# A state-space layer and feed-forward layer on one core: the round loop written out, and GpSimd's normalisation by two whole-tile operations

## The chip, the cores and the metric

One core of a Trainium2 chip runs the whole program. The metric is the device time of one execution in microseconds (us), the median over repeated runs. An execution is also profiled once; its span runs from the first to the last instruction.

## What is computed

The input has 32 sequences of 256 tokens with 128 features, all in 32-bit floats. Cut to what matters, the reference is:

```python
def _layernorm(x, axis=-1, eps=1e-05):
    m = jnp.mean(x, axis=axis, keepdims=True)
    v = jnp.var(x, axis=axis, keepdims=True)
    return (x - m) / jnp.sqrt(v + eps)
...
            def step(h, inp):
                dt_t, Bt, Ct, xt = inp
                dA = jnp.exp(dt_t[..., None] * A)
                h = dA * h + (xt * dt_t)[..., None] * Bt[:, None, :]
                y = jnp.einsum('bdn,bn->bd', h, Ct)
                return (h, y)
...
        h = jax.nn.silu(_tlin(x, w1_w, w1_s)) * _tlin(x, w2_w, w2_s)
        h = jax.nn.gelu(_tlin(h, h1_w, h1_s), approximate=False)
        h = jax.nn.gelu(_tlin(h, h2_w, h2_s), approximate=False)
        return _tlin(h, w3_w, w3_s)
    x = L0_attn_x
    x = _layernorm(x + _L0_attn_ref(x, ...), axis=-1)
    x = _layernorm(x + _L0_ffn_ref(x, ...), axis=-1)
```

The first half (`_L0_attn_ref`) projects each token to 256 channels and a gate z, runs a causal convolution of four taps and a silu, derives B, C and a step size dt per token, runs the scan `step` over time with 16 states for each of 256 channels, gates the sum with silu(z) and projects back to 128. The second half is a gated layer of width 512, two hidden layers of 512 and a last projection. A layer norm follows each half. The two layer norms are what the second part of the change touches.

## The kernel before, in words

The 8192 tokens are cut into 16 blocks of 512 (`NB` = 16, two sequences each). A block passes through a software pipeline of rounds; `run(j, par, scan, intake, front, back, tail)` is written once for each engine and issues that engine's part of round j. Round j does five things side by side, each switched by a flag:

- scan of block j: 32 tiles of channel and state in 16 steps v of two. ScalarE makes dA by an exponential (L337), VectorE multiplies (L593, U) and scans (L600, hb), GpSimd multiplies by C (L322, pb), TensorE adds the products up in PSUM by transposes (L692, Y).
- intake of block j+2: projection (L655), the convolution's first tap (ScalarE, L347) and the others (VectorE, L542).
- front of block A = j+1: silu, rows of B and C to DRAM and their broadcast back by DMAs on SyncE's queue, and dt: ScalarE (L380, L386, L388), then GpSimd's addition `add_dt` (L260) at step 11, then GpSimd's product xd (L266) and ScalarE's copy of it into the bank X (L343).
- back of block F = j-1: gate, output projection, residual r1 (VectorE, L616), the first layer norm, the transpose of its result x1 (TensorE, L744), the copy x1T (ScalarE, L488), the gated layer and the first hidden layer (TensorE L711, L714, L707).
- tail of block T = j-2: second hidden layer, last projection (L729), residual r2 (VectorE, L641), the second layer norm, the store of yo by SyncE (L238).

Every engine runs its own instructions in order, and the order around the change is written by hand: each `if v == ...` says at which step of the scan a piece stands. All dependencies are semaphores. A `wait_ge` stands ahead of the instruction that needs it and holds all that follows on that engine.

**The loop.** `rounds(eng, run)` (L164) calls `run` for rounds 0 and 1 with Python numbers, then opens a hardware loop `eng.Fori` of (16 - 4) / 2 = 6 turns with two rounds each (rounds 2 to 13), then rounds 14 to 17 written out. In the loop j is a register, so the numbers that are waited for are computed from it. There are five jumps from a turn's end back to its beginning, after rounds 3, 5, 7, 9 and 11, and each engine makes its own.

**The normalisation.** A block's layer norm works on a tile of 128 partitions x 4 rows (`NT` = 4, for a partition's four tokens) x 128 features. VectorE makes mean and variance (`stats`, L557 and L562, into mv). GpSimd's `normalise` (L283) then calls `rsqrt` (add eps, L279; power -0.5, L281), waits for its result, and works through the four rows one by one: each is one `tensor_scalar` (L288) that subtracts the mean and multiplies by the scale, both of them one number for each partition. It is called at step 4 of a round for block F (result x1, wanted by TensorE's `turn_x1` at step 5), and at step 10 for block T (result yo, wanted by the store). In round 17 VectorE normalises the last block itself (L634), so GpSimd does 31 normalisations.

What stands behind the step-10 call on GpSimd: the product of step 10, `add_dt` at step 11, the product of step 11. ScalarE waits for `add_dt` ahead of the first gelu (L399) of step 12.

Of the kernel before, what the change touches and what calls it, by code (L numbers as in the profile page):

```python
# [10 lines left out]
P = 128  # L11
# [25 lines left out]
def build(nc, xT, xtok, win, wx, chp, wout, w1, w2, h1, h2, w3, scales, w3s, ident_in, out):  # L37
    with ExitStack() as ctx:
# [6 lines left out]
        def sem(name):  # L45
            return ctx.enter_context(nc.semaphore(name))
# [58 lines left out]
        s_win, s_chp, s_ident, s_wx, s_weights = (sem("s_win"), sem("s_chp"), sem("s_ident"), sem("s_wx"),  # L105
                                                  sem("s_weights"))
        s_b0, s_pre0, s_soft0, s_dt0 = sem("s_b0"), sem("s_pre0"), sem("s_soft0"), sem("s_dt0")
        s_ready = sem("s_ready")
        s_zero, s_aexp, s_aneg, s_w3s = (sem("s_zero"), sem("s_aexp"),
                                                        sem("s_aneg"), sem("s_w3s"))  # L110
        s_xT, s_xtok = sem("s_xT"), sem("s_xtok")
# [12 lines left out]
        s_ga, s_sg, s_up, s_upc, s_hid = sem("s_ga"), sem("s_sg"), sem("s_up"), sem("s_upc"), sem("s_hid")  # L124
        s_h1, s_g1, s_h2, s_g2, s_w3 = sem("s_h1"), sem("s_g1"), sem("s_h2"), sem("s_g2"), sem("s_w3")
        s_w3t, s_r2t = sem("s_w3t"), sem("s_r2t")
        s_r2, s_l2, s_rs2, s_yo, s_out = sem("s_r2"), sem("s_l2"), sem("s_rs2"), sem("s_yo"), sem("s_out")

        def halves(x):
# [31 lines left out]
        def bank_in(b, c):  # L161
            return BIN_EARLY[c] if isinstance(b, int) and b < 2 else BIN[c]

        def rounds(eng, run):  # L164

            run(0, 0, True, True, True, False, False)
            run(1, 1, True, True, True, True, False)
            with eng.Fori(0, (NB - 4) // 2) as i:  # L170
                run(i * 2 + 2, 0, True, True, True, True, True)
                run(i * 2 + 3, 1, True, True, True, True, True)
            run(NB - 2, 0, True, False, True, True, True)
            run(NB - 1, 1, True, False, False, True, True)
            run(NB, 0, False, False, False, True, True)
            run(NB + 1, 1, False, False, False, False, True)
# [3 lines left out]
        @block.sync  # L180
        def _(sp):
            def load_xT(b):
                sp.dma_start(xT_sb[:], xT[:, bass.ts(b, TB)]).then_inc(s_xT, 16)

            def store_rows(b, par):
                sp.wait_ge(s_rows, b + 1)
                for t in range(NT):
                    sp.dma_start(rows_of(par, t), rows[t * 2 * NS:(t + 1) * 2 * NS, :]).then_inc(s_store, 16)

            def broadcast(b, par, q):  # L190
                piece = scr[par:par + 1, q * QN * TB:(q + 1) * QN * TB]
                sp.dma_start(flat(bbc[:, q * QN:(q + 1) * QN, :]), piece.to_broadcast([P, QN * TB])).then_inc(s_bbc[q], 16)

            def broadcast_C(b, par, q):
                piece = scr[par:par + 1, (NS + q * QN) * TB:(NS + (q + 1) * QN) * TB]
                sp.dma_start(flat(cbc[:, q * QN:(q + 1) * QN, :]), piece.to_broadcast([P, QN * TB])).then_inc(s_cbc[q], 16)

            load_xT(0)
            sp.dma_start(wx_sb[:], wx.rearrange("(c p) m -> p c m", p=P)).then_inc(s_wx, 16)
            sp.dma_start(ident[:], ident_in).then_inc(s_ident, 16)  # L200
            sp.dma_start(sc_sb[:], scales).then_inc(s_weights, 16)
            sp.dma_start(wout_sb[:], wout.rearrange("(c p) m -> p c m", p=P)).then_inc(s_weights, 16)
            sp.wait_ge(s_ip, 2)
            sp.wait_ge(s_z, 2)
            load_xT(1)
            sp.wait_ge(s_rows, 1)
            for t in range(0, NT, 2):
                sp.dma_start(rows_of(0, t), rows[t * 2 * NS:(t + 1) * 2 * NS, :]).then_inc(s_store, 16)
            sp.wait_ge(s_store, 16 * NT)
            for n, s_part in ((0, s_b0), (2, s_bbc[0])):  # L210
                piece = scr[0:1, n * TB:(n + 2) * TB]
                sp.dma_start(flat(bbc[:, n:n + 2, :]), piece.to_broadcast([P, 2 * TB])).then_inc(s_part, 16)
            broadcast_C(0, 0, 0)
            for q in range(1, NQ):
                broadcast(0, 0, q)
                broadcast_C(0, 0, q)
            sp.dma_start(w1_sb[:], w1).then_inc(s_weights, 16)
            sp.dma_start(w2_sb[:], w2).then_inc(s_weights, 16)
            sp.dma_start(h1_sb[:], h1.rearrange("(c p) m -> p c m", p=P)).then_inc(s_weights, 16)
            sp.dma_start(h2_sb[:], h2.rearrange("(c p) m -> p c m", p=P)).then_inc(s_weights, 16)  # L220
            sp.dma_start(w3_sb[:], w3.rearrange("(c p) m -> p c m", p=P)).then_inc(s_weights, 16)
            sp.dma_start(w3s_sb, w3s.to_broadcast([P, DM])).then_inc(s_weights, 16)

            def run(j, par, scan, intake, front, back, tail):
                first = isinstance(j, int) and j == 0
                I, A, F, T = j + 2, j + 1, j - 1, j - 2
                if scan and not first:
                    sp.wait_ge(s_u, TILES * j)
                    broadcast(j, par, NQ - 1)
                    sp.wait_ge(s_p, STEPS * j)  # L230
                    broadcast_C(j, par, NQ - 1)
                if intake:
                    sp.wait_ge(s_ip, 2 * A + 2)
                    sp.wait_ge(s_z, 2 * A + 2)
                    load_xT(I)
                if tail:
                    sp.wait_ge(s_yo, T + 1)
                    sp.dma_start(out[bass.ts(T, TB), :].rearrange("(t p) m -> p t m", p=P), yo[:]).then_inc(s_out, 16)  # L238
                if scan and back:
                    sp.wait_ge(s_r1, F + 1)  # L240
                if front:
                    store_rows(A, 1 - par)
                    sp.wait_ge(s_store, 16 * NT * A + 16 * NT)
                if scan:
                    sp.dma_start(xtok_sb[:], xtok[bass.ts(j, TB), :].rearrange("(t p) m -> p t m", p=P)).then_inc(s_xtok, 16)
                if front:
                    for q in range(NQ - 1):
                        sp.wait_ge(s_u, TILES * j + TILES // 2 + QN * (q + 1))
                        broadcast(A, 1 - par, q)
                        sp.wait_ge(s_p, STEPS * j + HALF + QN // 2 * (q + 1))  # L250
                        broadcast_C(A, 1 - par, q)

            rounds(sp, run)
            sp.wait_ge(s_out, 16 * NB)

        @block.gpsimd
        def _(pool):
# [22 lines left out]
                pool.wait_ge(s_rs, 2 * b + 1)  # L280
                nc.gpsimd.tensor_tensor(rs[:], ve[:], mhalf[:], ALU.pow).then_inc(s_rs, 1)  # L281

            def normalise(o, r, mv, ve, rs, s_l, s_rs, s_o, b):  # L283
                rsqrt(mv, ve, rs, s_l, s_rs, b)
                pool.wait_ge(s_rs, 2 * b + 2)
                pool.sem_inc(s_ready, 1)
                for t in range(NT):
                    last = nc.gpsimd.tensor_scalar(o[:, t, :], r[:, t, :], mv[:, t, 0:1], rs[:, t:t + 1],  # L288
                                                   ALU.subtract, ALU.mult)
                last.then_inc(s_o, 1)  # L290

            nc.gpsimd.memset(mhalf[:], -0.5).then_inc(s_zero, 1)
            nc.gpsimd.memset(eps[:], EPS).then_inc(s_zero, 1)
# [3 lines left out]
            def run(j, par, scan, intake, front, back, tail):  # L297
                first = isinstance(j, int) and j == 0
                I, A, F, T = j + 2, j + 1, j - 1, j - 2
                for v in range(STEPS):  # L300
                    if v == 4 and back:
                        normalise(x1[:, 1 - par, :, :], r1[:, 1 - par, :, :], mv1, ve1, rs1, s_l1, s_rs1, s_x1, F)
                    if v == 10 and tail:
                        if isinstance(j, int) and j == NB + 1:
                            rsqrt(mv2, ve2, rs2, s_l2, s_rs2, T)
                            continue
                        normalise(yo, r2, mv2, ve2, rs2, s_l2, s_rs2, s_yo, T)
                    if v in (7, 8) and back:
                        for m in range(2 * (v - 7), 2 * (v - 7) + 2):
                            pool.wait_ge(s_sg, 4 * F + 1 + m)  # L310
                            pool.wait_ge(s_upc, 4 * F + 1 + m)
                            nc.gpsimd.tensor_tensor(hid[:, m, :], hid[:, m, :], up[:, m, :], ALU.mult).then_inc(s_hid, 1)  # L312
                    if v == 2 and scan:
                        times_dt(j, par, 1)
                    if v == 11 and front:
                        add_dt(A, 1 - par)
                    if v == 13 and front:
                        times_dt(A, 1 - par, 0)
                    if scan:
                        c, n = output_term(j, v, first)  # L320
                        hs, qs = 2 * (v % H_PAIRS), 2 * (v % P_PAIRS)
                        nc.gpsimd.tensor_tensor(pb[:, qs:qs + 2, :], hb[:, hs:hs + 2, :], cbc[:, n:n + 2, :],  # L322
                                                ALU.mult).then_inc(s_p, 1)

            rounds(pool, run)

        @block.scalar
        def _(act):
# [198 lines left out]
                    if v == 15 and front:  # L527
                        fill_X(A, 0)

            rounds(act, run)  # L530

        @block.vector
        def _(dve):
# [113 lines left out]
                    if v == 14 and intake:  # L647
                        taps(I, 1)

            rounds(dve, run)  # L650

        @block.tensor
        def _(pe):
# [221 lines left out]
                        hidden(BH2[1], h2_sb, 1, g1, s_g1, s_h2, F)  # L875
                        hidden(BH2[2], h2_sb, 2, g1, s_g1, s_h2, F)

            rounds(pe, run)


# [32 lines left out]
```

## Time and profile before

| | |
|---|---|
| median of 3 runs | 1143.42 us (1143.41 to 1145.57) |
| time of the profiled execution | 1143.2 us |
| span of the profiled execution | 1141.4 us |
| mean granted TensorE clock | 0.968 |
| bytes moved by DMA | 152.13 MB |

How to read it: the profiled execution took 1143.2 us, 1.8 us more than its span from first to last instruction, and it stands 0.2 us below the median of the three runs. In the views PE is TensorE's matmuls, PEld its weight loads, DVE VectorE, ACT ScalarE, POOL GpSimd, SP SyncE. L and a number is a line of the kernel. An arrow in brackets names what ended the idle time before an instruction; "issue" means that the profile shows nothing it waited for. A tile's name carries no buffer number, and views of tiles that share memory show one name for all (g stands for g1 and for the softplus buffers in it, hid also for g2, r for r1, x1, r2 and yo).

### The profile page before, as it was taken

What the parts mean: (1) busy time and instruction counts of PE and PEld (TensorE: products, weight loads), DVE (VectorE), ACT (ScalarE), POOL (GpSimd) and SP (SyncE); (2) the same over time, 40 slices, a digit from 0 to 9 for tenths busy, and PEclk for the clock granted to TensorE, in tenths of its full rate; (3) what the DMA queues carried; (4) which work ended last, traced back from release to release, by engine and by line L of the source; (5) the groups of instructions that cost most, each with busy time, mean ns of one, the idle gap of its engine ahead of it and who ended that gap; (6) DMA issues with size and microseconds to landing.
All of it is one profiled execution on the core that took longest, in us unless ns stands there. A gap on an engine that the chain in (4) does not pass through costs nothing.

```text
span 1141.4 us, 16943 instructions
## 1 busy us (share of the span) xinstructions
PE 1034.3 (91%) x4928; PEld 646.8 (57%) x4928; DVE 1030.4 (90%) x1484; ACT 903.7 (79%) x1257; POOL 887.5 (78%) x561
## 2 busy tenths in 40 slices
PE   4655999999999999999989999999999999998997
PEld 2434566565656556565655656565565656555543
DVE  4999999998999989999899989999899999989511
ACT  7664989888898978989798888889789798978231
POOL 1667878889697978979698887978789797889640
PEclk8677999999999999999999999999999999999999
DMA  5661340705216070522507062250705225070000
GB/s 182 265 244 71 134 173 10 315 11 230 96 63 252 14 311 9 219 106 88 229 9 315 9 243 84 82 233 13 313 9 215 109 87 229 12 305 2 18 10 10
DMA packets 44065, 152.13 MB, mean 133 GB/s; under 512 B 4560, under 2 KB 24016, under 8 KB 27728
## 3 DMA queue, kind: packets, MB, share of 16 engines
q1 hardware_dynamic: 43600, 151.02, 33.8%
q14 instruction: 66, 0.54, 0.1%
q8 instruction: 15, 0.25, 0.1%
q10 hardware_dynamic: 384, 0.32, 0.1%
HBM read 146.08 MB, written 5.24 MB: 133 GB/s over the span
## 4 chain that ended last, share of the span: by engine, by line
PE 56%; issue 15%; ACT 11%; POOL 9%; DVE 7%; DMA 1%; POOLq 0%; ACTq 0%; DVEq 0%
PE G L707 26%; PE Y L692 11%; POOL pb L322 5%; ACT dA L337 5%; PE G L714 3%; DVE hb L600 3%; ACT g L380 3%; PE G L729 3%; PE Y L655 2%; PE G L675 2%; PE G L711 2%; DVE U L593 2%; POOL r L288 2%; PE Y L737 1%; PE G L659 1%
## 5 line engine op out<-in xcount | busy, mean ns | idle before, releaser
L322 POOL TENSOR_TENSOR pb<-hb,cbc 128x1024 f32<-128x1024 f32 x256 | 602.0, 2363 | 165.8 <-DVE hb L600 165.8
L600 DVE TENSOR_TENSOR_SCAN hb<-dA,U 128x512 f32<-128x512 f32 x512 | 594.6, 1204 | 0.0
L337 ACT ACTIVATE dA<-dt,negA 128x510 f32<-128x510 f32 x512 | 343.6, 713 | 95.5 <-DVE hb L600 73.1
L593 DVE TENSOR_TENSOR U<-X,bbc 128x512 f32<-128x512 f32 x512 | 327.0, 685 | 28.8 <-issue 19.0
L692 PEld LDWEIGHTS Y<-ident,pb 128*128 128x128 f32 x2048 | 241.8, 145 | 122.8 <-issue 70.9
L692 PE MATMUL Y<-ident,pb 128*128 128x128 f32 x2048 | 271.5, 280 | 39.5 <-POOL pb L322 39.4
L707 PE MATMUL G<-hid,h_sb 128*128 128x512 f32 x512 | 234.1, 601 | 2.3 <-ACT g L399 1.6
L707 PE MATMUL G<-g,h_sb 128*128 128x512 f32 x512 | 229.8, 593 | 0.0
L707 PEld LDWEIGHTS G<-hid,h_sb 128*128 128x128 f32 x512 | 96.6, 194 | 113.4 <-issue 108.3
L707 PEld LDWEIGHTS G<-g,h_sb 128*128 128x128 f32 x512 | 92.6, 190 | 94.5 <-issue 91.5
L288 POOL TENSOR_SCALAR r<-r,mv,rs 128x128 f32<-128x128 f32 x124 | 96.8, 794 | 6.6 <-POOL rs L281 6.6
L312 POOL TENSOR_TENSOR hid<-hid,g 128x512 f32<-128x512 f32 x64 | 80.3, 1275 | 7.1 <-ACT g L496 7.1
L399 ACT ACT_TABLE_LOAD x58 | 74.4, 1283 | 1.0
L337 ACT ACT_TABLE_LOAD x57 | 73.1, 1283 | 2.2 <-DVE hb L600 1.2
L399 ACT ACTIVATE hid<-G,sc_sb 128x512 f32<-128x512 f32 x64 | 41.8, 686 | 31.6 <-PE G L707 31.3
L399 ACT ACTIVATE g<-G,sc_sb 128x512 f32<-128x512 f32 x64 | 40.9, 685 | 30.9 <-POOL dt L260 15.8
L542 DVE SCALAR_TENSOR_TENSOR conv<-Y,chp_sb,conv 128x510 f32<-128x510 f32 (+2 forms) x84 | 62.1, 739 | 2.0
L655 PE MATMUL Y<-xT_sb,win_sb 128*128 128x512 f32 x56 | 33.6, 684 | 31.4 <-ACT gT L394 26.2
L729 PE MATMUL G<-w_sb,hid 128*128 128x128 f32 x480 | 56.7, 276 | 3.4 <-ACT hid L399 3.4
L729 PEld LDWEIGHTS G<-w_sb,hid 128*128 128x128 f32 x480 | 55.4, 192 | 6.8 <-ACT hid L399 3.4
L714 PE MATMUL G<-x1T,w_sb 128*128 128x512 f32 x96 | 50.4, 606 | 1.1 <-ACT hid L493 0.2
L711 PE MATMUL G<-x1T,w_sb 128*128 128x512 f32 x96 | 50.6, 609 | 0.7 <-ACT x1T L488 0.7
(90 smaller groups left out, 952.0 us busy)
## 6 DMA issues: line engine op xcount, KB each, us to landing
cbc<-scr SPq DMA_DIRECT2D x64, 1024.0 KB, 9.4
bbc<-scr SPq DMA_DIRECT2D x63, 1024.0 KB, 9.9
xT_sb<-xT_d SPq DMA_DIRECT2D x16, 256.0 KB, 2.8
xtok_sb<-xtok_d SPq DMA_DIRECT2D x16, 256.0 KB, 2.8
out_d<-r SPq DMA_DIRECT2D x16, 256.0 KB, 2.4
h_sb<-h_d SPq DMA_DIRECT2D x2, 1024.0 KB, 22.6
bbc<-scr SPq DMA_DIRECT2D x2, 512.0 KB, 4.8
scr<-rows SPq DMA_DIRECT2D x62, 16.0 KB, 1.5
```

The costliest lines, as they stand in the source:

```text
L288: last = nc.gpsimd.tensor_scalar(o[:, t, :], r[:, t, :], mv[:, t, 0:1], rs[:, t:t + 1], ALU.subtract, ALU.mult)
L312: nc.gpsimd.tensor_tensor(hid[:, m, :], hid[:, m, :], up[:, m, :], ALU.mult).then_inc(s_hid, 1)
L322: nc.gpsimd.tensor_tensor(pb[:, qs:qs + 2, :], hb[:, hs:hs + 2, :], cbc[:, n:n + 2, :], ALU.mult).then_inc(s_p, 1)
L337: nc.scalar.activation(halves(dA[:, u % DA_RING, :])[:, :, 1:SEQ], halves(dt[:, par, c, :])[:, :, 1:SEQ], ACT.Exp, scale=negA[:, c, n:n + ...
L399: nc.scalar.activation(o[:, m, :], banks[m], ACT.Gelu, scale=sc_sb[:, kind, m:m + 1]).then_inc(s_done, 1)
L593: nc.vector.tensor_tensor(U[i][:], X[:], bbc[:, n + i, :], ALU.mult).then_inc(s_u, 1)
L600: nc.vector.tensor_tensor_scan(hb[:, 2 * (v % H_PAIRS) + i, :], dA[:, u % DA_RING, :], U[i][:], 0.0, ALU.mult, ALU.add).then_inc(s_h, 1)
L692: last = nc.tensor.matmul(Y[c][:, t, :], tile_of(pb[:, 2 * (v % P_PAIRS) + i, :], t), ident[:], is_transpose=True, start=False, stop=(n + ...
L707: last = nc.tensor.matmul(to, w[:, k, m * P:(m + 1) * P], x[:, k, :], start=(k == 0), stop=(k == NH - 1))
L711: nc.tensor.matmul(BGATE[m], w1_sb[:, m * P:(m + 1) * P], x1T[:], start=True, stop=True).then_inc(s_ga, 1)
L714: nc.tensor.matmul(BUP[m], w2_sb[:, m * P:(m + 1) * P], x1T[:], start=True, stop=True).then_inc(s_up, 1)
L729: last = nc.tensor.matmul(tile_of(BW3, t), tile_of(g2[:, k, :], t), w3_sb[:, k, :], start=(k == 0 and t == 0), stop=(k == NH - 1), skip_gr ...
```

## The change

It does two things.

First, `rounds` loses its engine argument, and the hardware loop becomes a Python `for`: rounds 2 to 13 are written out for each engine as rounds 0, 1 and 14 to 17 were, with numbers in place of register values in every wait and address.

Second, `normalise` issues the subtraction for the whole tile right behind the power (mean broadcast over the 128 features), then waits for the power and for the subtraction, and then multiplies the whole tile by the broadcast scale, in place. Four `tensor_scalar` of 128x128 become two `tensor_tensor` of 128x512. Two semaphores (`s_cent1`, `s_cent2`) come in, and `s_ready`, which nothing waited for, goes with its increment.

```diff
-        s_ready = sem("s_ready")
...
+        s_cent1, s_cent2 = sem("s_cent1"), sem("s_cent2")
...
-        def rounds(eng, run):
+        def rounds(run):
             run(0, 0, True, True, True, False, False)
             run(1, 1, True, True, True, True, False)
-            with eng.Fori(0, (NB - 4) // 2) as i:
+            for i in range((NB - 4) // 2):
                 run(i * 2 + 2, 0, True, True, True, True, True)
                 run(i * 2 + 3, 1, True, True, True, True, True)
...
-            def normalise(o, r, mv, ve, rs, s_l, s_rs, s_o, b):
+            def normalise(o, r, mv, ve, rs, s_l, s_rs, s_c, s_o, b):
                 rsqrt(mv, ve, rs, s_l, s_rs, b)
+                nc.gpsimd.tensor_tensor(o[:], r[:], mv[:, :, 0:1].to_broadcast([P, NT, DM]), ALU.subtract).then_inc(s_c, 1)
                 pool.wait_ge(s_rs, 2 * b + 2)
-                pool.sem_inc(s_ready, 1)
-                for t in range(NT):
-                    last = nc.gpsimd.tensor_scalar(o[:, t, :], r[:, t, :], mv[:, t, 0:1], rs[:, t:t + 1],
-                                                   ALU.subtract, ALU.mult)
-                last.then_inc(s_o, 1)
+                pool.wait_ge(s_c, b + 1)
+                nc.gpsimd.tensor_tensor(o[:], o[:], rs[:].unsqueeze(2).to_broadcast([P, NT, DM]), ALU.mult).then_inc(s_o, 1)
...
-                        normalise(x1[:, 1 - par, :, :], r1[:, 1 - par, :, :], mv1, ve1, rs1, s_l1, s_rs1, s_x1, F)
+                        normalise(x1[:, 1 - par, :, :], r1[:, 1 - par, :, :], mv1, ve1, rs1, s_l1, s_rs1, s_cent1, s_x1, F)
...
-                        normalise(yo, r2, mv2, ve2, rs2, s_l2, s_rs2, s_yo, T)
+                        normalise(yo, r2, mv2, ve2, rs2, s_l2, s_rs2, s_cent2, s_yo, T)
...
-            rounds(pool, run)
+            rounds(run)
```

The last edit is made for all five engines' programs.

## Rows read from the trace of the kernel before

**Rows 1.** The page's head and its busy time of each engine.

```profile
span 1141.4 us, 16943 instructions
PE 1034.3 (91%) x4928; PEld 646.8 (57%) x4928; DVE 1030.4 (90%) x1484; ACT 903.7 (79%) x1257; POOL 887.5 (78%) x561
```

**Rows 2.** Waits, whole run: who waited for what, us, times, longest.

```profile
ACT dA L337 <- issue: 20.8, 5, 4.6
DVE U L593 <- issue: 19.0, 5, 4.0
...
ACT g L399 <- POOL dt L260: 15.8, 13, 1.8
```

**Rows 3.** Timeline of TensorE: start, duration, and in brackets the idle before.

```profile
133.61 1.10 PE L655 MATMUL Y<-xT_sb,win_sb 128*128 128x512 f32 x2 [2.02 <-ACT gT L394]
...
198.22 1.10 PE L655 MATMUL Y<-xT_sb,win_sb 128*128 128x512 f32 x2 [2.02 <-ACT gT L394]
...
262.82 1.10 PE L655 MATMUL Y<-xT_sb,win_sb 128*128 128x512 f32 x2 [2.01 <-ACT gT L394]
...
330.47 1.10 PE L655 MATMUL Y<-xT_sb,win_sb 128*128 128x512 f32 x2 [2.02 <-ACT gT L394]
...
462.78 1.70 PE L655 MATMUL Y<-xT_sb,win_sb 128*128 128x512 f32 x2 [2.02 <-ACT gT L394]
...
529.08 1.10 PE L655 MATMUL Y<-xT_sb,win_sb 128*128 128x512 f32 x2 [2.02 <-ACT gT L394]
...
928.80 1.10 PE L655 MATMUL Y<-xT_sb,win_sb 128*128 128x512 f32 x2 [2.02 <-ACT gT L394]
```

**Rows 4.** Stretches: length, PE, PEld, DVE, ACT, POOL busy; granted clock; DMA share, GB/s.

```profile
203.00:268.00 65.00, 62.86 (x314) 39.98 (x313) 64.54 (x93) 57.37 (x81) 56.24 (x37) 1.00 0.36 144
198.30:201.50 3.20, 3.20 (x8) 1.51 (x9) 3.20 (x5) 3.17 (x5) 3.20 (x5) 1.00 0.00 0
463.20:466.40 3.20, 3.20 (x5) 1.33 (x4) 3.20 (x5) 3.17 (x5) 3.20 (x5) 0.50 0.00 0
```

**Rows 5.** Timeline of ScalarE ahead of a TensorE gap, round 2.

```profile
193.61 2.76 ACT L380 ACTIVATE g<-G,chp_sb 128x512 f32<-128x512 f32 x4
...
197.49 0.59 ACT L394 ACTIVATE gT<-Y 128x512 f32<-128x512 f32 x1
```

**Rows 6.** All waits of VectorE from 152 to 283 us (rounds 2 and 3).

```profile
DVE r L616 <- PE Y L737: 0.6, 1, 0.6
DVE U L593 <- ACT X L343: 0.4, 1, 0.4
```

**Rows 7.** Instruction groups: busy us, mean ns of one, idle before.

```profile
L288 POOL TENSOR_SCALAR r<-r,mv,rs 128x128 f32<-128x128 f32 x124 | 96.8, 794 | 6.6 <-POOL rs L281 6.6
L312 POOL TENSOR_TENSOR hid<-hid,g 128x512 f32<-128x512 f32 x64 | 80.3, 1275 | 7.1 <-ACT g L496 7.1
...
L281 POOL TENSOR_TENSOR rs<-ve,mhalf 128x4 f32<-128x4 f32 x32 | 32.9, 1029 | 2.5
...
L608 DVE TENSOR_TENSOR w_sb<-w_sb,r 128x512 f32<-128x512 f32 x1 | 2.5, 2549 | 0.0
```

**Rows 8.** Timeline of round 3: x1 on GpSimd and its reader on TensorE.

```profile
236.04 3.12 POOL L288 TENSOR_SCALAR r<-r,mv,rs 128x128 f32<-128x128 f32 x4 [0.21 <-POOL rs L281]
...
241.63 0.60 PE L744 MATMUL Y<-ident,r 128*128 128x128 f32 x4
```

**Rows 9.** Timeline of round 2: GpSimd's dt and the gelu that waits for it.

```profile
203.11 2.35 POOL L260 TENSOR_TENSOR dt<-g 128x1024 f32<-128x1024 f32 x1
...
205.50 1.27 ACT L399 ACTIVATE g<-G,sc_sb 128x512 f32<-128x512 f32 x2 [0.98 <-POOL dt L260]
```

**Rows 10.** Timeline of rounds 14 and 15: where the chain passes through GpSimd.

```profile
1000.83 1.27 ACT L399 ACTIVATE g<-G,sc_sb 128x512 f32<-128x512 f32 x2 [1.79 <-POOL dt L260]
...
1048.15 1.09 PE L692 MATMUL Y<-ident,pb 128*128 128x128 f32 x8 [2.19 <-POOL pb L322]
...
1062.19 0.86 PEld L692 LDWEIGHTS Y<-ident,pb 128*128 128x128 f32 x8 [0.84 <-POOL pb L322]
```

More of the change, by code:

```diff
@@ L251, in run @@
                         broadcast_C(A, 1 - par, q)
-            rounds(sp, run)
+            rounds(run)
             sp.wait_ge(s_out, 16 * NB)
@@ L323, in run @@
                                                 ALU.mult).then_inc(s_p, 1)
-            rounds(pool, run)
+            rounds(run)
         @block.scalar
@@ L528, in run @@
                         fill_X(A, 0)
-            rounds(act, run)
+            rounds(run)
         @block.vector
@@ L648, in run @@
                         taps(I, 1)
-            rounds(dve, run)
+            rounds(run)
         @block.tensor
@@ L876, in run @@
                         hidden(BH2[2], h2_sb, 2, g1, s_g1, s_h2, F)
-            rounds(pe, run)
+            rounds(run)
 def kernel(L0_attn_x, L0_attn_W_in, L0_attn_conv_w, L0_attn_conv_b, L0_attn_W_x, L0_attn_A_log, L0_attn_D_param,
```

## The prediction

> **What bounds the kernel now.** I read the busy times first. TensorE and VectorE are both busy for 90% of the span, GpSimd for 78% [rows 1]. So two engines are nearly full, and time can be gained only where both stand still or where one of them is slowed.
>
> The waits of the whole run come next. VectorE and ScalarE each have exactly five idle times that nothing in the profile released, 19.0 us and 20.8 us together, so about 3.8 us and 4.2 us each [rows 2]. The loop has five back jumps. The idle times stand at those places: the first instruction of rounds 4, 6, 8, 10 and 12.
>
> Then I followed one TensorE instruction that stands once in each round, the input projection L655. It always follows a gap of 2.02 us. From 133.61 to 198.22 and from 198.22 to 262.82 it comes every 64.6 us [rows 3]. The first of these steps ends round 1, which is already written out, and the second lies in the loop: register values in the waits cost nothing. From 262.82 to 330.47 there is a back jump between, and it takes 67.65 us, 3.05 more. From 462.78 to 529.08 there is no back jump, and yet it takes 66.30 us, 1.70 more. There L655 itself took 1.70 us in place of 1.10.
>
> What makes that second delay is in the stretches. Behind the gap at 198 the granted clock was 1.00, behind the gap at 462 it was 0.50, the lower of the two levels (1.2 GHz), for some 3.2 us [rows 4]. Before the fall TensorE had done nothing but stand in its 2.02 us gap. The timeline shows such a fall behind four of the 13 gaps, the one at 462 being the first. Three cost 1.7 us each, and one was swallowed by the back jump that followed it.
>
> Last, what sets 64.6 us. In a whole round TensorE is busy 62.86 of 65 us [rows 4], and with the 2.02 us gap that is all of it. The gap is ScalarE's: before it copies gT for TensorE it works off four softplus activations (2.76 us) and two exponentials [rows 5]. VectorE waits 0.6 and 0.4 us in two rounds [rows 6], so it would need 64.3. The steady round is a ring of TensorE and ScalarE, with VectorE 0.3 us behind as the next bound. GpSimd is not in it.
>
> **Part 1, the loop.** It removes five back jumps on each engine. From the first L655 to the last are 928.80 - 133.61 = 795.2 us and 12 rounds [rows 3]. Twelve undisturbed rounds take 12 x 64.605 = 775.3 us. The difference of 19.9 us is everything that the loop and the clock cost TensorE: three falls of the clock at 1.7 are 5.1 us, and the rest, 14.8 us, is five back jumps at 2.96. A jump costs TensorE less than VectorE's 3.8, because TensorE lags by a little at each turn's end and catches up.
>
> Written out, nothing takes the jumps' place, I say. More code has to be fetched, but round 1 is written out and the first pass through rounds 2 and 3 is code met for the first time; VectorE waits there for X and for TensorE only, with no idle time of the "issue" kind [rows 6], and the round takes the same 64.6 us. So the jumps' term is -14.8 us. Its bounds are zero (the stall moves elsewhere) and the 19.0 us of VectorE.
>
> **Part 2, the normalisation.** It removes four row operations of 794 ns; they run as one piece of 3.12 us behind a wait of 0.21 us for the power [rows 7, 8]. It adds two operations on 128x512. The trace has no broadcast operand on GpSimd. The nearest row is the product of two 128x512 tiles, same engine, same operation, same size: 1275 ns [rows 7]. The lower bound is one row operation's 794 ns; the upper one is 2549 ns, the one operation with a broadcast operand (on VectorE, two SBUF inputs) in the trace. I take 1275, the nearest in kind. The subtraction starts behind the power without a wait, and the product waits 0.21 us for it. Before: 0.21 + 3.12 = 3.33 us. After: 1.27 + 0.21 + 1.27 = 2.75 us. The gain is 0.58 us a call, 31 calls, 18 us of GpSimd's time. With the bounds a call gains 1.5 us or loses 2.0 us.
>
> Of a rule that speaks against this: row operations have one tile input, the new ones two, and the row says 794 ns for 128 elements of one input, 1275 ns for 512 of two, so the row form pays mostly per instruction and per scalar operand. The Trainium skill (GPSIMD Engine Reference, Engine selection) calls two-input elementwise work about half as fast as VectorE's and one-input work roughly line-rate. By that rule one would not trade; the measured 794 ns is far from line rate, so the trace disagrees and decides, and the sum stays.
>
> On the path this gains nothing in the steady rounds. x1 is ready at 239.16, and TensorE reaches its transpose at 241.63, 2.5 us later [rows 8]. The store of yo is awaited by nobody near. The call at step 10 delays dt, for which ScalarE waits 0.98 us in round 2 and 15.8 us over 13 rounds [rows 2, 9]; that wait gets shorter by 0.58 each, but ScalarE then has less to catch up and meets the same TensorE ring. In the last rounds, where no intake fills VectorE, the chain does pass here: ScalarE waits 1.79 us for dt in round 14, TensorE then 2.19 us for pb, and 0.84 us for pb behind the step-10 call of round 15 [rows 10]. The first pair gains 0.58 us, the last 0.58. Term: -1.2 us (bounds 0 and -2.3, by the lower price: 1.5 from the dt path, 0.84 from the last).
>
> **The clock.** The five back jumps go, the 2.02 us gap of each round stays, 13 times. Four of 13 gaps brought a fall, none of the first five. Bounds: 0, and four at 1.7 = 6.8 us. I take two, 3.4 us: with no back jumps no fall is swallowed, but the long quiet stretch at the beginning is the one that looks like the new kernel throughout. The Trainium skill (TensorE: Matmul & The Clock Gate, Why this matters for your kernels) has as a rule that only longer idle gaps than these bring the clock down; by it this term would be 0 and the total 3.4 us less. The rows show falls behind gaps of 2.02 us, so here the trace disagrees with it.
>
> **Sum.** 1141.4 - 19.9 - 1.2 + 3.4 = 1123.7 us of span. With the 1.8 us around it, 1125.5 us. The profiled execution lay 0.2 us below the median of the runs shown, so no correction. About 0.2% (2.3 us) is what a measurement of this kernel can tell from no change.
>
> **The rivals.**
>
> (a) *The dear broadcast: slower.* If a step of zero costs GpSimd what the upper bound says, 2549 ns, the call at step 10 takes 2.0 us more than before, and dt, ScalarE's gelus and its copy into X come 2.0 us later in each round. VectorE waits for X at the round's start (0.4 us already) [rows 6]; it has 0.3 us of slack against the ring, so the round grows by some 1.7 us. Over 13 rounds that is 22 us, and the last rounds lose 2.4 where they should gain 1.2: 1125.5 + 22 + 4 = 1151. It decides from about 2.4 us for one whole-tile operation, where the growth eats what the jumps gave. For it: no such operand in the trace. Against: the product of two full tiles takes 1275 ns [rows 7], and nothing suggests that re-reading one number takes longer than reading 512. Chance 0.04.
>
> (b) *The stall is not the jump's.* If the 3.8 us belong to fetching instructions at all, the written-out kernel pays them as often, only elsewhere. Then only -1.2 is left, 1142. For it: nothing tells the two apart inside one idle time. Against: the first pass is free of it. Chance 0.03.
>
> (c) *The gap falls into step with the clock.* Every round is now the same, so if one gap brings a fall, all may: 13 x 1.7 = 22 in place of 3.4, so 1144. Against: five steps in a row of exactly 64.6 or near show none. Chance 0.03. A milder form, five to eight falls, gives 1131 to 1136, chance 0.05.
>
> (d) *VectorE catches the ring.* ScalarE relieved by 0.58 us at step 12 ends the gap earlier, and the round shrinks to VectorE's 64.3: 13 x 0.3 = 4 us less, 1121.5. Chance 0.1.
>
> **How the numbers follow.** The forecast, with none to four falls of the clock, holds 0.75: 1122.1 to 1128.9, with the tail's bounds 1121 to 1130. With (d), without falls, the low end is 1119. The range 1120 to 1131 leaves out (a), (b), (c) and the milder form, and the edge of (d), less than 2 in 10. Faster: the forecast, (d) and the milder form of (c), 0.90. Same: (b) and (c), 0.06. Slower: (a), 0.04.
>
> **What would show it.** Right: no "issue" idle on VectorE and ScalarE at round starts; L655 every 64.6 us, or 66.3 behind a fall; L288's successors at some 1.27 us each, GpSimd's busy time down by 18 us; ScalarE's wait for dt near 0.4 us in round 2. Wrong: idle of the "issue" kind scattered over written-out rounds (b), X waited for by 2 us a round (a), a clock of 0.5 behind most gaps (c), a period below 64.6 (d).

## The result and the profile after

| kernel | median us | runs | range | ratio to before, 95% interval |
|---|---|---|---|---|
| before | 1144.05 | 4 | 1143.41 to 1145.57 | |
| changed | 1126.18 | 4 | 1124.17 to 1127.29 | 0.984 (0.9821 to 0.9859) |
| forecast | 1125.5 | | 1120 to 1131 | |

The change saves 17.9 us. The profiled execution of the changed kernel took 1125.33 us with a span of 1123.5 us; the sum had been made for 1123.7 us of span.

Head and busy times of the changed kernel's page:

```profile
span 1123.5 us, 14735 instructions
PE 1028.0 (92%) x4928; PEld 649.0 (58%) x4928; DVE 1029.9 (92%) x1484; ACT 901.6 (80%) x1257; POOL 854.8 (76%) x499
```

Against [rows 1], TensorE, VectorE and ScalarE do the same work in 18 us less. GpSimd issues 62 instructions fewer on data and is busy 32.7 us less, not the 18 us that I had forecast. The instruction groups say why (count, busy us, mean ns, idle before):

```profile
L281 POOL TENSOR_TENSOR rs<-ve,mhalf 128x4 f32<-128x4 f32 x32 | 32.4, 1012 | 2.5
L285 POOL TENSOR_TENSOR r<-r,mv 128x512 f32<-128x512 f32 x31 | 32.3, 1042 | 0.0
L288 POOL TENSOR_TENSOR r<-r,rs 128x512 f32<-128x512 f32 x31 | 32.2, 1039 | 4.5
```

A whole-tile operation with a broadcast operand takes 1040 ns, less than the 1275 ns of a product of two full tiles [rows 7]. A call costs 1.04 + 0.14 + 1.04 = 2.2 us behind the power in place of 3.3.

VectorE's waits over the whole run of the changed kernel:

```profile
DVE r L614 <- PE Y L735: 8.9, 14, 3.5
...
DVE U L591 <- ACT X L341: 6.4, 5, 2.7
...
DVE r L632 <- issue: 1.4, 1, 1.4
```

The five idle times of 3.8 us [rows 2] are gone, and nothing of their kind appears in the written-out rounds (the 1.4 us at L632 is the last normalisation's, and was there before). TensorE's timeline at the input projection, which is now L653:

```profile
132.32 1.10 PE L653 MATMUL Y<-xT_sb,win_sb 128*128 128x512 f32 x2 [2.01 <-ACT gT L392]
...
196.92 1.10 PE L653 MATMUL Y<-xT_sb,win_sb 128*128 128x512 f32 x2 [2.02 <-ACT gT L392]
...
455.31 1.95 PE L653 MATMUL Y<-xT_sb,win_sb 128*128 128x512 f32 x2 [2.02 <-ACT gT L392]
...
521.61 1.10 PE L653 MATMUL Y<-xT_sb,win_sb 128*128 128x512 f32 x2 [2.01 <-ACT gT L392]
...
909.18 1.85 PE L653 MATMUL Y<-xT_sb,win_sb 128*128 128x512 f32 x2 [2.01 <-ACT gT L392]
```

From 132.32 to 196.92 a round takes 64.60 us, and so do ten more. One takes 66.30, from 455.31 to 521.61, and there the projection took 1.95 us. The granted clock over stretches behind the two slow projections, and behind a wait in round 15 (length, busy times, clock, DMA):

```profile
455.50:458.70 3.20, 3.20 (x4) 1.20 (x4) 3.20 (x4) 3.17 (x5) 3.06 (x3) 0.50 0.30 85
909.40:912.60 3.20, 3.20 (x5) 1.14 (x5) 3.20 (x4) 3.17 (x5) 3.06 (x3) 0.50 0.30 88
1029.10:1032.30 3.20, 3.20 (x10) 2.24 (x10) 3.20 (x4) 3.20 (x6) 3.20 (x3) 0.50 0.00 0
```

Three falls to the lower level, two of them behind the 2.02 us gap, the third behind a wait of 2.49 us for pb.

**Where the 17.9 us of span came from.** The input projection cuts the span into four pieces. Its first row is that of round 0, in the kernel before and in the changed one:

```profile
62.76 1.10 PE L655 MATMUL Y<-xT_sb,win_sb 128*128 128x512 f32 x2
...
61.99 1.10 PE L653 MATMUL Y<-xT_sb,win_sb 128*128 128x512 f32 x2
```

- Up to round 0's projection, 0.8 us less. No normalisation has run by then, as GpSimd's first power starts at 105.06 and 104.43 us, and the other runs have this row anywhere from 61.84 to 64.09. So these 0.8 us are chance, and no part of the change.
- From there to round 1's projection, 70.3 us in place of 70.9, 0.5 less. This is GpSimd's part: the two other kernels with the old normalisation and TensorE's old order take 70.86 too, and those with the new one, without added powers and in that order, 70.19 to 70.34.
- The twelve rounds up to the last projection, 776.9 us in place of 795.2, 18.3 less [rows 3].
- From there to the end, 214.3 us in place of 212.6, 1.7 more. The written-out kernel with the old normalisation takes 213.9 here, with one fall of the clock, in round 15. Three kernels with the new normalisation and that one fall (TensorE, ScalarE, or GpSimd and SyncE loop) take 212.7. So the fall in round 15 costs 1.3 us and GpSimd's part gives back 1.2; the other 1.6 us are the changed kernel's second fall behind the gap, at 909.4.

### The profile page after: what moved, and what is told of

Read it like the earlier page. It is cut to its first block, busy times and chain, and to the rows that moved or that the text cites. A ratio compares the mean times of both kernels' runs of the same rounds, so it can differ in the third digit from the quotient of the medians.

```text
span 1123.5 us, 14735 instructions
## 1 busy us (share of the span) xinstructions
PE 1028.0 (92%) x4928; PEld 649.0 (58%) x4928; DVE 1029.9 (92%) x1484; ACT 901.6 (80%) x1257; POOL 854.8 (76%) x499
## 4 chain that ended last, share of the span: by engine, by line
PE 69%; ACT 16%; DVE 7%; issue 6%; POOL 2%; DMA 0%; ACTq 0%; DVEq 0%; POOLq 0%
PE G L705 33%; PE Y L690 14%; ACT dA L335 6%; PE G L727 4%; PE G L712 3%; ACT g L378 3%; DVE hb L598 3%; PE G L673 2%; PE Y L653 2%; PE Y L735 2%; PE G L657 2%; DVE U L591 2%; PE G L709 1%; ACT L351 1%; ACT xs L351 1%
## 5 line engine op out<-in xcount | busy, mean ns | idle before, releaser
L690 PEld LDWEIGHTS Y<-ident,pb 128*128 128x128 f32 x2048 | 244.1, 145 | 111.0 <-issue 73.0
L690 PE MATMUL Y<-ident,pb 128*128 128x128 f32 x2048 | 272.1, 280 | 31.9 <-POOL pb L320 31.9
L653 PE MATMUL Y<-xT_sb,win_sb 128*128 128x512 f32 x56 | 32.3, 661 | 31.0 <-ACT gT L392 26.2
L392 ACT ACTIVATE gT<-Y 128x512 f32<-128x512 f32 x32 | 19.0, 595 | 33.1 <-PE Y L698 33.1
```

Source lines behind the costliest of these rows:

```text
L690: last = nc.tensor.matmul(Y[c][:, t, :], tile_of(pb[:, 2 * (v % P_PAIRS) + i, :], t), ident[:], is_transpose=True, start=False, stop=(n + ...
```

## The experiments

Twelve kernels ran. The ratio is always to the kernel before on the same chip; the medians come from several chips, on which the kernel before took 1143.0 to 1144.2 us.

| run | median us | ratio, 95% interval |
|---|---|---|
| written out, old normalisation | 1126.67 | 0.9855 (0.9838 to 0.9873) |
| loop, new normalisation | 1142.80 | 0.9994 (0.9985 to 1.0003) |
| loop of three turns, old normalisation | 1133.07 | 0.9904 (0.989 to 0.9918) |
| changed, gap filled | 1116.78 | 0.9758 (0.9744 to 0.9771) |
| changed, VectorE loops | 1144.10 | 1.0005 (0.9995 to 1.0014) |
| changed, TensorE loops | 1126.37 | 0.9857 (0.984 to 0.9873) |
| changed, ScalarE loops | 1126.78 | 0.986 (0.9843 to 0.9876) |
| changed, GpSimd and SyncE loop | 1126.71 | 0.9857 (0.9841 to 0.9874) |
| changed, call 2.0 us longer | 1134.08 | 0.9914 (0.9899 to 0.9929) |
| changed, call 4.0 us longer | 1179.42 | 1.0317 (1.0292 to 1.0342) |
| loop, new normalisation, gap filled | 1135.98 | 0.9933 (0.9918 to 0.9948) |
| written out, old normalisation, gap filled | 1118.78 | 0.9781 (0.9768 to 0.9795) |

### The two halves of the change alone

Rounds written out, `normalise` as before:

```diff
-            with eng.Fori(0, (NB - 4) // 2) as i:
+            for i in range((NB - 4) // 2):
```

> The rounds are written out, the normalisation stays as it was (four row operations). Theory (the gain is the five back jumps, and GpSimd's gain counts only where the chain passes through it): the changed kernel's 1126.2 us plus 1.1 us in the first rounds, where TensorE waits for x1 (2.4 us after, 3.5 us before), plus about 1.3 us on the dt path of round 14, so some 1128.6 us; with one fall of the clock more or less 1127 to 1131. L655 every 64.60 us, no idle of the issue kind at round starts. Rival (GpSimd's 33 us of saved time matter in every round): well above, 1134 us or more, and a period over 64.6.

Measured 1126.67 us, 1.9 below the expectation and 0.3 below its range. The period is 64.60 us. The rival falls: 33 us of GpSimd's time saved do not count in the rounds.

The new `normalise` in the kernel before, loop kept:

> The loop stays, only the normalisation is the new one. Theory: the before's 1144.05 us less 1.1 in the first rounds and 1.3 in the last, 1141.6 us, range 1139 to 1143.5; the five idle times of VectorE and ScalarE at the back jumps stay at 3.8 and 4.2 us each. Rival (GpSimd's time matters in every round): 1136 us or less. Rival (the broadcast operand slows others): above 1144 us.

Measured 1142.80 us against 1144.20 of the kernel before on the same chip, 1.4 us less, with 1.0 inside the interval of the ratio. VectorE waits "issue: 19.5, 5, 4.0" as before. So nearly all of the 17.9 us is the loop. The normalisation is worth 0.5 to 1.4 us in this kernel by the medians, which hardly separate that from nothing, and 1.7 us by the traces (0.5 in the first rounds, 1.2 in the last).

### Fewer jumps with the same loop

```diff
-            with eng.Fori(0, (NB - 4) // 2) as i:
-                run(i * 2 + 2, 0, True, True, True, True, True)
-                run(i * 2 + 3, 1, True, True, True, True, True)
+            with eng.Fori(0, (NB - 4) // 4) as i:
+                for k in range(4):
+                    run(i * 4 + 2 + k, k % 2, True, True, True, True, True)
```

> The kernel before, but its loop has three turns of four rounds in place of six turns of two: two back jumps in place of five, the same instructions. Theory (each back jump costs TensorE 2.96 us): 3 x 2.96 = 8.9 us less than the kernel before, 1135.2 us, range 1132 to 1138, with two idle times of the issue kind on VectorE of 3.8 us. Rival (fetching instructions costs by the amount of code, whether jumped over or not): 1144 us or more, the 19 us of idle time spread over more places.

Measured 1133.07 us. By the medians, two jumps cost 6.4 us against the written-out kernel with the old normalisation, 3.2 each; against the kernel before, three jumps fewer give 11.1 us, 3.7 each. The waits of this kernel:

```profile
DVE U L593 <- issue: 8.5, 2, 4.5
...
ACT dA L337 <- issue: 7.7, 2, 3.9
```

Two jumps, two idle times. The rival of a cost that goes with the amount of code falls: the turn is twice as long, and VectorE's idle time at a jump is 4.0 and 4.5 us, little more than the 3.8 of the shorter turn. That it is the jump is now shown; what the engine does in those 4 us was not looked into.

The medians hide how the sum is made up, since falls of the clock are in both terms. In the trace of this kernel the projection steps over the two jumps take 69.16 and 69.20 us, 4.6 over 64.60. Behind each jump TensorE waits for pb, 2.65 and 2.70 us, and then the clock falls (0.50 from 416.3 to 419.5 us and from 679.2 to 682.4). Behind none of its 13 gaps of 2.02 us does it fall.

### Which engine's jump it is

In four kernels one engine (or two) kept the hardware loop while the others ran written-out rounds:

```diff
-        def rounds(run):
+        def rounds(eng, run, name):
...
-            for i in range((NB - 4) // 2):
-                run(i * 2 + 2, 0, True, True, True, True, True)
-                run(i * 2 + 3, 1, True, True, True, True, True)
+            def turn(i):
+                run(i * 2 + 2, 0, True, True, True, True, True)
+                run(i * 2 + 3, 1, True, True, True, True, True)
+
+            if name in ('dve',):
+                with eng.Fori(0, (NB - 4) // 2) as i:
+                    turn(i)
+            else:
+                for i in range((NB - 4) // 2):
+                    turn(i)
```

> The changed kernel, with the hardware loop kept on VectorE alone; the four other engines run written-out rounds. Theory (VectorE's jump is the one that costs, since it has only 0.33 us a round to spare): five idle times of 3.8 us on VectorE, each 3.0 us on the time, so 1126.2 + 15 = 1141 us, range 1138 to 1143. Rival (the cost comes from all engines stalling at once, and one alone is absorbed): under 1131 us.

Measured 1144.10 us, ratio 1.0005: the whole gain of the change is gone, and the time lies 1.1 us above the range. The five steps over a jump are 14.7 us over 64.60 together, as expected; the rest is the clock, which falls behind five of the 13 gaps (two in the changed kernel). The waits of VectorE in this kernel:

```profile
DVE U L598 <- issue: 19.2, 5, 4.1
```

> The changed kernel, with the hardware loop kept on TensorE alone. Theory (TensorE showed no idle time at the jumps of the kernel before): 1126 us, range 1124 to 1128.5. Rival (its stall was hidden there behind VectorE's and is as long, and TensorE is the fullest engine): five times 3 us, 1141 us.

Measured 1126.37 us. TensorE's jump costs nothing here.

> The changed kernel, with the hardware loop kept on ScalarE alone. Theory (ScalarE's exponentials run up to six tiles ahead of VectorE, and a tile takes VectorE 1.8 us, so 4.2 us of idle time are covered on VectorE's side): five idle times of some 4.2 us on ScalarE and 1126 to 1129 us. Rival (the ring of TensorE and ScalarE stretches by the stall): 1138 us or more.

Measured 1126.78 us. Two rows of the timeline at the second jump, VectorE's and ScalarE's (lines are shifted by the edit):

```profile
415.89 2.32 DVE L605 TENSOR_TENSOR_SCAN hb<-dA,U 128x512 f32<-128x512 f32 x2
...
416.20 2.55 ACT L342 ACTIVATE dA<-dt,negA 128x510 f32<-128x510 f32 x4 [5.25 <-issue]
```

ScalarE stands for 5.25 us, and VectorE scans on with no bracket, from exponentials made ahead. At the four other jumps ScalarE stands for 4.5 to 4.8 us; there the profile puts the end of the idle time down to VectorE's scan. ScalarE stands longer than VectorE did, and it costs almost nothing.

> The changed kernel, with the hardware loop kept on GpSimd and SyncE. Theory (GpSimd idles 8 us a round and SyncE waits most of the time): 1126 us, range 1124 to 1129. Rival (GpSimd's jump is the 6.8 us of issue time that the chain of the kernel before showed at each jump on GpSimd's queue): 1136 us or more, with TensorE waiting for pb behind each jump.

Measured 1126.71 us. The 6.8 us "issue" pieces on GpSimd's queue, which the chain of the kernel before shows at each jump, were no cause: GpSimd was waiting for VectorE's scan anyway.

So it may be enough to write out VectorE's program. This is argued from the four kernels: one in which all the other engines loop together was not run. The idle times of ScalarE and VectorE look alike in [rows 2]; only VectorE's counts.

### The gap of 2.02 us filled

TensorE's step 10, in the changed kernel:

```diff
-                    if v == 10 and intake:
-                        pe.wait_ge(s_xT, 16 * I + 16)
-                        pe.wait_ge(s_gts, 2 * j + 1)
-                        in_proj(I, 0)
                     if v == 10 and back:
                         if front:
                             pe.wait_ge(s_rows, A + 1)
                         hidden(BH1[1], h1_sb, 1, hid, s_hid, s_h1, F)
+                    if v == 10 and intake:
+                        pe.wait_ge(s_xT, 16 * I + 16)
+                        pe.wait_ge(s_gts, 2 * j + 1)
+                        in_proj(I, 0)
```

> The changed kernel, and TensorE's program at step 10 has the 16 matmul instructions' worth of the first hidden layer's second tile ahead of the input projection, so that the 2.02 us gap that waits for ScalarE's copy is filled. Theory (the gap is part of the 64.60 us ring and is what brings the clock down): the round falls to VectorE's 64.27 us, 13 x 0.33 = 4.3 us less, and the two falls of the clock go, 3.4 us less: 1126.2 - 7.7 = 1118.5 us, range 1116 to 1121; clock 1.00 through rounds 1 to 13. Rival (the ring closes through another wait, the input projection's reader on ScalarE): period 64.6 us again and 1123 to 1126 us, with a new wait of ScalarE or TensorE of some 2 us. Rival (the falls have nothing to do with the gap): falls remain, 1122 us.

Measured 1116.78 us, 9.4 us less than the changed kernel and 27.4 less than the kernel before on the same chip. It is the best version of this study. TensorE's projection and a round's stretch in this kernel:

```profile
262.62 1.02 PE L653 MATMUL Y<-xT_sb,win_sb 128*128 128x512 f32 x2
...
903.79 1.02 PE L653 MATMUL Y<-xT_sb,win_sb 128*128 128x512 f32 x2
```

```profile
265.00:330.00 65.00, 63.94 (x311) 39.77 (x310) 64.70 (x94) 57.90 (x82) 54.47 (x33) 1.00 0.36 145
```

No wait stands before it, ten rounds take 641.2 us, 64.12 each, and VectorE has no wait at all between 152 and 900 us. From 117 us, in round 1, the granted clock stays at 1.00 up to a fall in round 15. The theory holds in both parts, ring and clock. VectorE's true need is 64.12 us, not the 64.27 that I had read off; [rows 6] says so too, as waits of 0.6 and 0.4 us in two rounds are 0.5 a round, and 64.6 - 0.5 = 64.1.

The same edit with the loop kept:

> The hardware loop on all engines with the new normalisation, and TensorE's gap filled as in the run with the filled gap. Theory (jumps cost VectorE 3.8 us each, now with no slack of TensorE's to catch up in, and the falls of the clock go): 1116.8 + 5 x 3.8 = 1136 us, range 1134 to 1138. Rival (the jumps cost the same 3.0 as before): 1132 us.

Measured 1135.98 us. Two projections in a row, with one jump between:

```profile
260.34 1.02 PE L653 MATMUL Y<-xT_sb,win_sb 128*128 128x512 f32 x2
...
328.70 1.02 PE L653 MATMUL Y<-xT_sb,win_sb 128*128 128x512 f32 x2
```

That step is 68.36 us, 4.24 over 64.12, and the five of them together are 19.9 us over, the whole of VectorE's idle 19.4. With the ring in place a jump cost 2.96; with VectorE as the only bound it costs all of its stall. Both numbers come from the same stall, seen through different slack. The other half of the theory, that the falls of the clock go, did not hold: with the gap filled the clock still falls behind three of the five jumps (at 291, 554 and 687 us), where TensorE waits 2.4 to 2.7 us for pb:

```profile
289.14 1.09 PE L690 MATMUL Y<-ident,pb 128*128 128x128 f32 x8 [2.71 <-POOL pb L320]
```

These falls cost little: the steps with one are 0.2 us longer on average than the two without.

### What a longer GpSimd call costs

Two further powers on a spare tile in each call, read by nothing:

```diff
                 rsqrt(mv, ve, rs, s_l, s_rs, b)
+                for k in range(2):
+                    nc.gpsimd.tensor_tensor(spare[:, k, :], ve[:], mhalf[:], ALU.pow)
                 nc.gpsimd.tensor_tensor(o[:], r[:], mv[:, :, 0:1].to_broadcast([P, NT, DM]), ALU.subtract).then_inc(s_c, 1)
```

> The changed kernel with two further powers of 128x4 in each normalisation, written to a spare tile and read by nothing: 2 x 1.01 = 2.0 us more on GpSimd a call, so that a call takes 1.0 us more than before the change. The prediction's model of its rival (a) (a later dt reaches VectorE through ScalarE's copy into X, of which VectorE can spare 0.33 us a round): 13 x 0.7 = 9 us over the kernel with the old normalisation, 1136 us. Rival (the delay of dt is absorbed in the written-out rounds, as GpSimd still idles, and only the first and last rounds show it): 1127 to 1130 us.

Measured 1134.08 us, 7.9 more than the changed kernel. VectorE's waits from 152 to 900 us:

```profile
DVE U L594 <- ACT X L344: 11.0, 12, 1.4
```

and the period is 65.13 us. The way is the one that rival (a) named: dt late (ScalarE waits 1.7 us for it each time, against 1.0 with the old normalisation), ScalarE's copy into X late, VectorE waiting about 0.9 us at each round's start. The rival of this run, that the delay is absorbed, falls.

With four powers:

> The same with four powers: 4.0 us more on GpSimd a call than in the changed kernel, 3.0 us more than before the change; GpSimd's busy time would be 980 us. The prediction's model: 13 x 2.7 = 35 us over the old normalisation, 1162 us. Rival (absorbed up to a point; x1 had 2.5 us to spare in round 3 before the change and now comes 0.5 us late for TensorE, and dt comes 3 us later to ScalarE): 0.5 to 2 us a round, 1133 to 1153 us.

Measured 1179.42 us, worse than either number. TensorE's timeline in round 6 shows what comes on top, and a stretch behind it the clock:

```profile
449.83 0.66 PE L745 MATMUL Y<-ident,r 128*128 128x128 f32 x4 [1.14 <-POOL r L291]
452.14 1.97 PE L693 MATMUL Y<-ident,pb 128*128 128x128 f32 x8 [1.65 <-POOL pb L323]
```

```profile
451.70:454.90 3.20, 2.76 (x10) 2.25 (x11) 3.20 (x5) 1.87 (x3) 3.20 (x3) 0.50 0.00 0
```

TensorE waits for x1 and at once again for pb, two idle times with 0.66 us of work between them, and the clock falls as the second one ends: from 451.6 us on once in each of ten rounds, 68.27 us apart, which is the period. The lockstep that rival (c) feared exists, though behind other idle times than its gap; it took a longer call to bring it on.

The falls are the smaller part of the cost. Between these two projections the clock does not fall:

```profile
337.56 1.10 PE L656 MATMUL Y<-xT_sb,win_sb 128*128 128x512 f32 x2 [2.01 <-ACT gT L395]
...
405.12 1.10 PE L656 MATMUL Y<-xT_sb,win_sb 128*128 128x512 f32 x2 [2.01 <-ACT gT L395]
```

That round takes 67.56 us, 2.96 over 64.60, near the 2.7 of the model; with a fall in each it is 68.27, another 0.7. My estimate from this one round: of the 53 us over the old normalisation some 38 (13 x 2.96) are the late dt and x1, some 7 the falls in the rounds. The remaining 8 us were not followed.

### The normalisation once the gap is filled

> Rounds written out, gap filled, and the old normalisation by four row operations. Theory (VectorE's 64.27 us round is the bound, GpSimd's calls lie beside it): 1116.8 us plus 0.5 to 1.5 us in the first and last rounds, 1117.3 to 1118.3 us. Rival (with the ring opened, GpSimd's later dt now counts in each round): 1121 us or more.

Measured 1118.78 us, 2.0 more than with the new normalisation, on another chip, but with ratios whose intervals meet only at their ends (0.9768 to 0.9795 against 0.9744 to 0.9771). The period is 64.38 in place of 64.12, and TensorE waits 12 times for pb between 152 and 900 us (9.8 us), not once with the new normalisation. So with the ring opened GpSimd's call counts a little in each round: less than the rival's 4 us, more than the theory's 1.5.

## Why the prediction was right

- **The loop, -19.9 us including the clock.** Right in size and place. The jumps' 14.8 us as a term cannot be read alone from the change, but the written-out kernel with the old normalisation gives 17.5 us, its falls of the clock included, and VectorE's five jumps alone bring back 14.7 us in the trace. What the prediction did not tell is that VectorE's jump alone does it. It named VectorE's slack of 0.33 us as the next bound (0.5 by its own rows) and then counted TensorE's delay; the four mixed kernels put it the right way round.
- **No new cost of the code.** Right: the first pass through rounds 2 and 3 was good evidence, and the changed kernel shows no idle time of the issue kind in a round.
- **The price of the broadcast.** 1040 ns in place of 1275; a call gains 1.1 us rather than 0.58. That was the term of which only the neighbours were known, and the nearest row was 23% too dear. The rule weighed there (the Trainium skill, GPSIMD Engine Reference, Engine selection) would have spoken against the trade; these rows speak for it.
- **GpSimd beside the path in steady rounds.** Right: 64.60 us with either normalisation. ScalarE's wait for dt went from 15.8 us in all to 0.5 (I had said 0.4 a round), and nothing came of it, since the ring closes elsewhere.
- **The last rounds, -1.2 us.** The first half of the term was right in kind: the wait for dt in round 14 is 0.46 us in place of 1.79 [rows 10], so it gained 1.3 and not 0.58. The second half was a misreading. The 0.84 us in [rows 10] is idle time of the weight loads, not of the matmuls. The matmuls before it, in the timeline of the kernel before:

```profile
1058.58 3.60 PE L707 MATMUL G<-hid,h_sb 128*128 128x512 f32 x8
1062.19 0.55 PE L692 MATMUL Y<-ident,pb 128*128 128x128 f32 x3
```

  The one ends at 1062.18 and the next begins at 1062.19. There was next to nothing to gain. The term still came out at 1.2 us, all of it from the first half: the number is right by luck.
- **The first rounds, left out.** In round 1 TensorE waits for x1, 3.5 us in the kernel before and 2.4 after, with the whole pipeline behind it. That is a place where GpSimd's call is on the path. Of its 1.1 us, 0.5 reach the projection of that round. The waits of the kernel before showed the place, and I had looked at steady rounds only.
- **The clock, +3.4 us.** Two falls behind the gap, as taken, and a third in round 15, which the term left out. That it was two was partly luck: the kernels with this gap in which VectorE runs written-out rounds have one fall behind it, or two; those in which VectorE loops have four, four, five and none (the loop of three turns). The filled gap shows that this term was the gap's: without it no fall comes between 120 us and round 14, with either normalisation. In all runs, each fall from 126 us up to round 14 stands at the end of an idle time of TensorE of 1.6 to 2.7 us, or less than 2 us behind it. The rule that the prediction weighed (the Trainium skill, TensorE: Matmul & The Clock Gate, Why this matters for your kernels) warns of longer gaps than these. But 1.9 us of transposes (L698, L681, L690 in the changed kernel) stand right ahead of each gap of 2.02 us, and no run separates the gap from them. The fall in round 15 is not the new normalisation's: the written-out kernel with the old one has it too, behind a wait of 2.20 us for pb, where the kernel before waited 2.19 us without a fall [rows 10].
- **The rivals.** (a) did not come, as the broadcast is cheap, but its mechanism was right: one microsecond over the old call costs about 7.5 us (9 was expected), three cost 53 (35 expected, which holds for the steady rounds and leaves out the falls and the ends). By a line between the two runs (1134.1 and 1179.4, with 1144), an estimate, the change would have gained nothing with a call some 2.4 us longer than the new one. (b) is ruled out by the changed kernel, which has no such idle time, and by the loop of three turns. (c) was not there in this kernel; with the longest call a fall did come in each round, at another place. (d) did not happen: relieving ScalarE at step 12 does not shorten the ring, moving TensorE's work into the gap does.

The sum was closer (0.2 us of span) than its parts deserve. The clock took 4.6 us (1.7, 1.6 and 1.3) where 3.4 was forecast, 1.2 more. GpSimd's part was 1.7 us (0.5 in the first rounds, 1.2 in the last) where 1.2 was forecast, and the start gave 0.8 us by chance, 1.3 together. The two errors cancel.

## What to carry to other kernels

When every engine stalls at a loop's end, ask which of them has slack of that length just there; the one without it sets the price, and its program is the first to write out. A steady period in which no engine is free of waits is a ring: look for the gap in it, and for the work of the waiting engine that can stand in it. An operand broadcast along a row lets one instruction do what a row of small ones did: here two whole-tile operations took 2.1 us and four row operations 3.1. Whether the small ones pay for their number or for their scalar operands, no run separates.

## What the runs showed of the hardware

- A jump back in a hardware loop left VectorE idle for 3.7 to 4.5 us and ScalarE for 3.4 to 6.4 with turns of two rounds or four. TensorE's jump cost nothing that the time shows (1126.37 us), nor did GpSimd's and SyncE's (1126.71).
- On GpSimd `tensor_tensor` on 128x512 takes 1275 ns with two full inputs and 1040 with one of them broadcast from one number per row; `tensor_scalar` with two scalar operands takes 794 ns for only 128x128; a power on 128x4 takes 1012 ns.
- TensorE's granted clock fell to 0.50 for some 3.2 us or a little more behind idle times of 1.6 to 2.7 us, not behind each of them: for the gap of 2.02 us, 4 of 13 in the kernel before, 2 of 13 after, and none once it was filled. With the loop kept and the gap filled, three falls stayed, behind waits of 2.4 to 2.7 us at the jumps.
